# A delta-rule layer in a vision tower: two accumulators for the output's sum, and a new order of the projections and transfers ahead of the recurrence

## What is computed

```python
q = silu(x @ Wq)                       # (b, n, h, hd)
k = silu(x @ Wk); k = k * rsqrt(sum(k * k, -1) + 1e-12)
v = x @ Wv
beta = 2.0 * sigmoid(x @ Wbet); a = sigmoid(x @ Wf)
def step(S, inp):                      # scan over the 64 tokens
    Sd = a * S
    u = v - k . Sd
    S = Sd + beta * outer(k, u)
    o = q . S
o = o * rsqrt(mean(o * o, -1) + 1e-6) * norm_w
return o @ Wo
```

## Time and profile before

| | us |
|---|---|
| median of three runs | 1399.51 (1390.93 to 1405.37) |
| the profiled execution | 1405.84, its span 1404.2 |
| last expert result, first row of this layer on DVE | 570.41, 576.43 |
| first DVE product of the recurrence (L1640) | 666.64 |
| last state ready, DVE's last-token product (L1652) | 962.46 |
| busy: PE, DVE, ACT, POOL | 1163.6, 807.8, 586.9, 521.8 |

### The profile page before, as it was taken

The page is one execution under the profiler, slowest core; times in us unless marked ns, Lnnn a source line. Parts: engine busy times, 40 slices in busy tenths (PEclk is TensorE's granted clock), DMA queues, the critical chain, the costliest instruction groups (busy, mean ns, idle before and its releaser), DMA issues. The chain is left out here.

```text
span 1404.2 us, 24940 instructions
## 1 busy us (share of the span) xinstructions
PE 1163.6 (83%) x9227; PEld 896.1 (64%) x9227; DVE 807.8 (58%) x1850; ACT 586.9 (42%) x1468; POOL 521.8 (37%) x565
## 2 busy tenths in 40 slices
PE   6999984799999999676788888885799999867854
PEld 4666663798999999432455656554577777645543
DVE  3666666211122221545989898996467767532886
ACT  3544452111212121254667667672234444424544
POOL 0111111232333332333687777873112222120657
PEclk9999995799999999899999999997699999979875
DMA  4111100898888886486000000002000031026601
GB/s 146 32 46 46 35 9 12 318 346 333 333 316 329 320 321 240 120 213 173 1 1 0 1 1 1 1 1 74 13 9 11 12 140 50 2 86 253 199 20 57
DMA packets 83352, 162.24 MB, mean 116 GB/s; under 512 B 44128, under 2 KB 62176, under 8 KB 77216
## 3 DMA queue, kind: packets, MB, share of 16 engines
q1 hardware_dynamic: 55536, 111.23, 23.2%
q0 software_dynamic: 10512, 45.10, 8.5%
q10 hardware_dynamic: 17184, 4.33, 1.5%
HBM read 134.28 MB, written 26.35 MB: 114 GB/s over the span
## 5 line engine op out<-in xcount | busy, mean ns | idle before, releaser
L1431 PEld LDWEIGHTS banks<-ys,ident 128*128 128x128 f32 x1008 | 127.3, 191 | 122.3 <-issue 118.3
L922 PE MATMUL banks<-rowsT,w_up 128*128 128x128 f32 x1716 | 202.5, 279 | 0.2 <-DMA w_up<-in_up_w 0.2
L922 PEld LDWEIGHTS banks<-rowsT,w_up 128*128 128x128 f32 x1716 | 199.3, 196 | 0.4 <-DMA w_up<-in_up_w 0.4
L1697 POOL TENSOR_TENSOR ys<-xT_d,q_by_time 128x1024 f32<-128x1024 f32 x63 | 149.0, 2364 | 63.7 <-ACT xT_d L1513 63.7
L1431 PE MATMUL banks<-ys,ident 128*128 128x64 f32 x1008 | 135.0, 289 | 44.7 <-ACT chain_o L1517 43.5
L1422 PE MATMUL banks<-made,ident 128*128 128x512 f32 x256 | 136.8, 616 | 14.6 <-DVE made L1645 14.5
L1542 ACT ACTIVATE banks<-banks,rate 128x256 f32<-128x256 f32 x256 | 104.0, 444 | 91.8 <-DVE made L1640 91.8
L1091 DVE TENSOR_TENSOR hT<-banks,silu 64x128 f32<-64x128 f32 x39 | 11.0, 283 | 170.5 <-ACT silu L979 170.5
L936 PE MATMUL banks<-w_down,hT 128*128 128x256 f32 x468 | 107.5, 379 | 0.6 <-DVE res L1101 0.6
L1640 DVE TENSOR_TENSOR made<-banks,ka 128x512 f32<-128x512 f32 x128 | 87.9, 687 | 23.6 <-PE banks L1422 20.9
L1643 DVE TENSOR_REDUCE banks<-made 128x32 f32<-128x544 f32 x128 | 93.2, 728 | 4.4
(11 more groups left out here) (313 smaller groups left out, 2349.2 us busy)
## 6 DMA issues: line engine op xcount, KB each, us to landing
w_up<-in_up_w SPq DMA_DIRECT2D x39, 1408.0 KB, 5.9
w_down<-in_down_w POOLq DMA_DIRECT2D x39, 768.0 KB, 5.4
inter<-res_x SPq DMA_DIRECT2D x16, 512.0 KB, 3.1
back<-inter SPq DMA_DIRECT2D x15, 512.0 KB, 3.9
patches<-in_patches SPq DMA_DIRECT2D x16, 384.0 KB, 3.2
f<-in_f SPq DMA_DIRECT2D x6, 1024.0 KB, 11.4
ys<-token_rows SPq DMA_DIRECT2D x16, 256.0 KB, 2.8
xn_rows<-xn_all SPq DMA_DIRECT2D x16, 128.0 KB, 1.7
```

Of the source, the lines that this page charges most:

```text
L922: ins = pe.matmul(out[:, m * P:(m + 1) * P], w[:, c, m * P:(m + 1) * P], x[:, c, :], start=(c == 0), stop=(c == 1))
L1431: ins = pe.matmul(o_sum, ident[:, :], products[t % 2][:, :, :, n], start=(n == 0), stop=(n == FOLDED - 1))
L1697: pool.tensor_tensor(qs[:, :, :, :], Sc[(t + 1) % 2][:, :, :, :], bcast(qt[:, t, :, :], 2, HD), ALU.mult).then_inc(sem("qs_made"), 1)
```

## The change

Nine edits, all around this layer:

- `o_sum` has two banks, 5 and 7, used in turns, and `sum_folded(t)` waits for `o_made` t-1 in place of t. The last chunk of squares moves to bank 6; DVE's `mean_square` waits for all three chunks.
- `ticks` goes; PE's and ACT's order are written out. Keys of group g+1 are projected ahead of the queries of group g.
- The first group is projected tile by tile (`project_tile`, 12 products of 128x128).
- The rates are computed in four pieces of 32 partitions, so that the bank holds 128x128 and not 32x512. One store and one load a group replace two and two.
- All stores go by SP, interleaved with the last row loads. ACT issues none.
- The root of the keys' sums is one POOL instruction on 128x64 (`root`, power -0.5), in place of eleven on DVE.
- `square_keys(3)` comes ahead of `turn_queries(2)` on ACT.
- The last group's values and queries are loaded by SP; its queries are turned by POOL (`last_turned`), for which DVE no longer waits at the start but at its last product.
- The rates' weights are interleaved on the host, and `rates` in DRAM is laid out to match.

```diff
-    rates = nc.dram_tensor("rates", (CG, 2, IMAGES // CG, HEADS, TOK), F32).ap()
+    rates = nc.dram_tensor("rates", (CG, IMAGES // CG, HEADS, 2, TOK), F32).ap()
...
-            "rate_made": sb("rate_made", [2 * HEADS, ng])}
+            "rate_made": sb("rate_made", [P, P])}
...
-    o_sum = banks[:, 5, 0:CG * HD].rearrange("p (g v) -> p g v", g=CG)
+    o_sum = [banks[:, b, 0:CG * HD].rearrange("p (g v) -> p g v", g=CG) for b in (5, 7)]
...
-        return banks[:, 6 + n // 2, CG * CUTS[n]:CG * CUTS[n + 1]].rearrange("p (g t) -> p g t", g=CG)
+        return banks[:, 6, CG * CUTS[n]:CG * CUTS[n + 1]].rearrange("p (g t) -> p g t", g=CG)
...
-        return banks[0:2 * HEADS, 1, :]
-
-    def ticks(steps, last):
-        for tick in range(last):
-            for lag, per, count, step in steps:
-                if tick >= lag and (tick - lag) % per == 0 and (tick - lag) // per < count:
-                    step((tick - lag) // per)
+        return banks[:, 1, 0:P]
...
+        def store_pair(first, g):
+            store_made(sp, g, first)
+            store_made(sp, g, first + 1)
+
+        def store_rates(g):
             sp.wait_ge(sem("rate_made"), g + 1)
-            for kind in range(2):
-                sp.dma_start(rates[g, kind, :, :, :].rearrange("b h t -> h b t"),
-                             rate_made[kind * HEADS:(kind + 1) * HEADS, :].rearrange("h (b t) -> h b t", t=TOK)
-                             ).then_inc(sem("rate_stored"), 16)
-            load_chain(sp, g, "k", k)
-            sp.wait_ge(sem("rate_stored"), 32 * g + 32)
-            for kind in range(2):
-                sp.dma_start(rate[:, g, kind, :], rates[g, kind, :, :, :].rearrange("b h t -> (b h) t")
-                             ).then_inc(sem(f"rates{g}"), 16)
-
+            sp.dma_start(rates[g].rearrange("(b j) h n t -> (j h n) b t", b=2),
+                         rate_made[:, :].rearrange("p (b t) -> p b t", b=2)).then_inc(sem("rate_stored"), 16)
+
+        def load_rates(g):
+            sp.wait_ge(sem("rate_stored"), 16 * g + 16)
+            sp.dma_start(rate[:, g, :, :].rearrange("p n t -> p (n t)"),
+                         rates[g].rearrange("b h n t -> (b h) (n t)")).then_inc(sem(f"rates{g}"), 16)
...
+        queries, keys, values = 0, 2, 4
         all_sent(sp)
         for t in range(YS):
             load_rows(t)
-        for t in range(T - YS):
+        for t in range(8):
             next_rows(t)
-        for g in range(CG):
-            send_keys(g)
+        store_pair(keys, 0)
+        next_rows(8)
+        store_pair(values, 0)
+        next_rows(9)
+        store_pair(queries, 0)
+        store_rates(0)
+        next_rows(10)
+        next_rows(11)
+        load_chain(sp, 0, "k", k)
+        load_rates(0)
+        store_pair(keys, 1)
...
+        store_pair(keys, 3)
+        store_rates(3)
+        store_pair(queries, 2)
+        load_chain(sp, 3, "k", k)
+        store_pair(values, 3)
+        load_rates(3)
+        store_pair(queries, 3)
+        load_chain(sp, 3, "v", v)
+        load_chain(sp, 3, "q", q)
...
+        def project_tile(t):
+            at = slice(t * P, (t + 1) * P)
+            pe.wait_ge(sem("xT_copied"), t + 1)
+            for m in (2, 3, 4, 5, 0, 1):
                 for c in range(DC):
                     ins = pe.matmul(banks[:, 2 + m, at], w[:, c, m * P:(m + 1) * P], xT[0][:, c, at],
                                     start=(c == 0), stop=(c == 1), skip_group_check=True)
-                if half:
...
+        def rate_sums(g, copied):
+            pe.wait_ge(sem("xT_copied"), copied)
+            if g:
+                pe.wait_ge(sem("rate_made"), g)
             for c in range(DC):
-                ins = pe.matmul(rate_bank(), w_rate[:, c, :], xT[g % 2][:, c, :], start=(c == 0), stop=(c == 1))
+                images = xT[g % 2][:, c, :].rearrange("p (b j t) -> p j b t", b=2, j=NT)
+                for j in range(NT):
+                    rows = slice(2 * HEADS * j, 2 * HEADS * (j + 1))
+                    ins = pe.matmul(rate_bank()[rows, :].rearrange("p (b t) -> p b t", b=2), w_rate[:, c, :],
+                                    images[:, j, :, :], start=(c == 0), stop=(c == 1), skip_group_check=True)
             ins.then_inc(sem("rate_sums"), 1)
...
-                if t:
-                    pe.wait_ge(sem("o_made"), t)
+                if t > 1:
+                    pe.wait_ge(sem("o_made"), t - 1)
             for n in range(FOLDED // 2 * h, FOLDED // 2 * (h + 1)):
-                ins = pe.matmul(o_sum, ident[:, :], products[t % 2][:, :, :, n], start=(n == 0),
+                ins = pe.matmul(o_sum[t % 2], ident[:, :], products[t % 2][:, :, :, n], start=(n == 0),
...
+        turn(0)
+        turn(1)
+        project_tile(0)
+        turn(2)
+        project_tile(1)
+        turn(3)
+        project_tile(2)
+        turn(4)
+        project_tile(3)
+        turn(5)
+        turn(6)
+        turn(7)
+        rate_sums(0, 8)
+        project(2, 1)
+        project(3, 1)
+        turn(8)
+        turn_past_rates(9, 0)
+        project(4, 1)
+        turn(10)
+        project(5, 1)
+        turn(11)
...
+        project(2, 3)
+        project(3, 3)
+        rate_sums(3, 16)
+        project(0, 2)
+        project(1, 2)
+        project(4, 3)
+        project(5, 3)
+        project(0, 3)
+        project(1, 3)
...
-                if first != 2:
-                    for m in (first, first + 1):
-                        store_made(act, g, m)
...
-            act.copy(o[:, :, :, t], o_sum).then_inc(sem("o_made"), 1)
+            act.copy(o[:, :, :, t], o_sum[t % 2]).then_inc(sem("o_made"), 1)
...
+        keys(3)
+        square_keys(2)
+        rates_of(3)
+        queries(2)
+        values(3)
+        turn_queries(1)
+        queries(3)
+        square_keys(3)
+        turn_queries(2)
...
-            once.mark(dve.tensor_scalar(n2[:, g, :], n2[:, g, :], 1e-12, None, ALU.add))
-            once.settle()
-            x, y = n2[:, g, :].bitcast(I32), rn[:, g, :].bitcast(I32)
-            once.mark(dve.tensor_scalar(y, x, 1, None, ALU.logical_shift_right))
-            once.settle()
-            once.mark(dve.tensor_scalar(y, y, -1.0, float(0x5F3759DF), ALU.mult, ALU.add))
-            once.settle()
-            for _ in range(3):
-                newton(n2[:, g, :], rn[:, g, :], tmp[:, g, :])
+            dve.tensor_scalar(n2[:, g, :], n2[:, g, :], 1e-12, None, ALU.add).then_inc(sem("k_summed"), 1)
...
+            dve.wait_ge(sem("k_root"), g + 1)
...
-            dve.wait_ge(sem("o_summed"), n + 1)
+            dve.wait_ge(sem("o_summed"), CHUNKS_O)
...
+        def root(g):
+            pool.wait_ge(sem("k_summed"), g + 1)
+            pool.tensor_tensor(rn[:, g, :], n2[:, g, :], minus_half[:, 0:1].to_broadcast([P, TOK]), ALU.pow
+                               ).then_inc(sem("k_root"), 1)
...
+        load_chain(pool, 2, "q", q)
+        root(3)
+        scale_keys(3)
+        pool.wait_ge(sem(f"chain_q{CG - 1}"), 16)
+        pool.tensor_copy(qt[:, :, CG - 1, :].rearrange("p t d -> p d t"), q[:, CG - 1, :, :]
+                         ).then_inc(sem("last_turned"), 1)
+        pool.wait_ge(sem("last_turned"), 1)
+        pool.wait_ge(sem("q_turned"), CG - 1)
...
-        "rate_w": rows(np.concatenate([a("L1_attn_Wbet"), a("L1_attn_Wf")], 1)),
+        "rate_w": rows(np.stack([a("L1_attn_Wbet"), a("L1_attn_Wf")], 2).reshape(D, 2 * HEADS)),
```

More of the change, by code:

```diff
@@ L1524, in square_out @@
                        o[:, :, :, CUTS[n]:CUTS[n + 1]]).then_inc(sem("o_squared"), 1)
-        ticks([(0, 1, T, norm), (1, 1, T, copy_xT), (5, 4, CG, made_of(2, ACT.Silu)), (5, 4, CG, rates_of),
-               (6, 4, CG, made_of(4, ACT.Copy)), (7, 4, CG, made_of(0, ACT.Silu)), (9, 4, CG, square_keys),
-               (12, 4, CG, turn_queries)], T + 9)
+        norm(0)
+        norm(1)
+        copy_xT(0)
+        norm(2)
+        copy_xT(1)
+        norm(3)
+        copy_xT(2)
+        norm(4)
+        copy_xT(3)
+        norm(5)
+        copy_xT(4)
+        norm(6)
+        keys(0)
+        copy_xT(5)
+        norm(7)
+        copy_xT(6)
+        copy_xT(7)
+        values(0)
+        rates_of(0)
+        queries(0)
+        norm(8)
+        norm(9)
+        keys(1)
+        copy_xT(8)
+        copy_xT(9)
+        norm(10)
+        norm(11)
+        copy_xT(10)
+        norm(12)
+        copy_xT(11)
+        values(1)
+        rates_of(1)
+        norm(13)
+        norm(14)
+        keys(2)
+        square_keys(0)
+        norm(15)
+        copy_xT(12)
+        rates_of(2)
+        queries(1)
+        copy_xT(13)
+        copy_xT(14)
+        square_keys(1)
+        copy_xT(15)
+        values(2)
+        turn_queries(0)
+        keys(3)
[7 more added lines that the diff above has]
+        turn_queries(2)
         act.preload_act_table_set("natural_log_exp_and_others")
@@ L1684, in gpsimd @@
         prepare(pool)
-        for g in range(CG):
-            if g:
-                scale_keys(g - 1)
```

(17 more changed lines are left out.)

100 lines of the change are left out of this document (55 added, 45 removed).

## The result

| | before | changed |
|---|---|---|
| median of 20 runs, us | 1399.29 (1390.93 to 1406.31) | 1393.81 (1388.27 to 1396.55) |
| ratio | | 0.9947 (0.9934 to 0.996) |
| the profiled execution, its span | 1405.84, 1404.2 | 1388.62, 1386.9 |
| first row of the layer | 576.43 | 572.37 |
| first DVE product | 666.64 | 675.30 |

The change gains 0.5%: 7.4 us by the ratio, 5.5 by the medians, where 33 were forecast. The time lies 8 us above the upper end of the range for 8 in 10 (1352 to 1386).

The account below looks back on a forecast made before the run. DVE, held up by PE's output sum, bounds the recurrence; PE and transfers alternate in the front. 1405.84 - 21.3 (banks) - 12.1 (front) = 1372.4, or 1366 us against 1399.51; own range 1356 to 1377, 8 in 10 1352 to 1386.

Parts of the forecast that it names:

- Two banks: Recurrence: PE's output sum no longer waits for ACT's copy, a step falls from 4.56 to 4.18 us; 21.3 us gained.
- deduction for the squares: Recurrence: four of nine steps with squares' sums keep their old period, taking 1.5 us off the banks' 22.8 us.
- the wait passes on to POOL: Rival, recurrence: PE's sum still waits for POOL's fold and half the gain stays, 1377 us; chance 0.08.
- little comes of it: Rival: front and recurrence both disappoint, or the bank's copy was not the step's limit; 1394 us, chance 0.06.
- The price of the root: Front's end: one POOL root on 64 columns takes 2.5 us, between 0.86 and 45, replacing DVE's 2.8 us.
- fourth rival: Front: POOL's root is paid by the column, four in a row delay the first product; 1457 us, chance 0.07.
- PE's end at 641: Front: PE's last projection product ends at 641 us, within 637.5 to 652.6.
- cost PE nothing: Front: the rates' pieces, eight products of 128 columns a group against two of 512, add no PE time.
- The hole and the half clock: Front: PE's 3.9 us idle before the second group and 2.8 us lost to lower clock, laid to ACT's stores, disappear.
- Transfers at 0.93: Front: 53.8 us of full DMA work from about 594.3 at a 0.93 share ends at 652.1; at 0.84, 658.4.
- Two floors of one height: Front's end: PE's path and the transfers both allow about 652; first product taken at 654.5, 12.1 us gained.
- The row loads: Front: SP's rows 13 to 15, behind stores, may come some 3 us late, but PE reaches them long after.

Follow-up runs that it names:

- e2: The kernel before with two banks for the output's sum and nothing else: 1379.71 us, ratio to before 0.9841.
- e5: e1 with POOL powers and products on 1 to 256 columns of scratch data added behind the recurrence: run once, 1436.1 us.
- e3: The kernel before with the keys' root as one POOL instruction in place of DVE's eleven, nothing else: 1419.44 us, ratio to before 1.0135.
- e1: The changed kernel with the keys' root back on DVE, all else kept: 1362.36 us, ratio to before 0.9736.
- e9: e1 with the last group's `kb` shared, 10 of 16 columns of each head on POOL and 6 on DVE: 1365.38 us, ratio to before 0.9734.
- e7: e1 with the first group projected in two halves again, not tile by tile: 1371.46 us, ratio to before 0.9783.
- e8: e1 with the last group's queries turned by ACT and waited for before the recurrence: 1369.87 us, ratio to before 0.9771.
- e6: e1 with the values' and queries' stores issued by ACT again: 1362.61 us, ratio to before 0.9716.
- e10: e1 with POOL's last `kb` computed twice, one after the other: 1369.98 us, ratio to before 0.9767.

## Why the prediction was wrong, step by step

- **Two banks: right.** 21.3 us forecast; the recurrence shows 21.6, and e2, the banks alone, 21.7. The deduction for the squares was too small: four steps were to keep their old period, and 8 keep a wait, at 4.6 to 4.9 us a step. The other 52 steps x 0.38 give 19.8, so some 2 of the 21.6 us came from elsewhere, and the total is nearer than its terms. The rivals "the wait passes on to POOL" and "little comes of it" fall: POOL is what PE's sum waits for, and DVE does not feel it.
- **The price of the root: wrong, and the cause of the miss.** "I take 2.5 us, nearer to the low end, since a single column carries the whole start of an instruction." It is 10.55 us. The one-column row is 0.71 us, of which about 0.16 is the column (e5), so most of it is a start, as I said; but a column's 0.16 us, 63 times over, is 10 us. I had bounds of 0.86 and 45 us, could not tell between them, and took a value at the low end with the words "nobody needs that many passes for a root". No row stood behind that. The edit alone, on the kernel before, costs 15.9 us of front (e3), and taken out of the changed kernel it gives back 28.4 (e1). By the factor of two that the Trainium skill ("GPSIMD Engine Reference", section on performance versus the Vector engine) gives for elementwise work, the estimate was 5.5 us: the right direction, and half of the cost.
- **The fourth rival's mechanism: right; the closeness of its date is luck.** It said 617 + 4 x root + 4 x 3.83 + 0.4. With 10.55 that is 674.9; the first product came at 675.30. But the first root began at 612.95 and not 617, and a root and its `kb` take 15.7 us and not 14.4, because DVE's scaling and POOL's issues of loads stand between them. The two errors, -4.1 and +4.5 us, cancel. Its break-even was 8.5 us for the front and 13.9 for the whole change, and 10.55 lies between: the front loses, the recurrence more than pays for it. The mechanism had a chance of 0.07, and I priced it only at 28 us a root, where it makes the kernel slower. The case that came, between the two limits, had no place among the rivals, though its sign ("if POOL's root is over 8 us, the fourth rival holds") was on the list. Two of its figures are off by little: the second break-even comes to 13.8, and the time at 28 us to 1456.
- **PE's end at 641: too late by 9.5 us.** It was 631.5. The layer began 4.1 us earlier (572.37); over all kernels that date ran from 570.0 to 576.4, and e1 and e9, alike up to there, began at 572.6 and 576.1, so it is no effect of the front's edits. Most of the rest can be the rates: "cost PE nothing" was wrong in the other direction. Their sum takes 0.64 us and not 1.90, 4 x 1.26 = 5.0 us in all. The hole and the half clock went as forecast; tiles brought about 1 us and not 3 (e7), so a further 2 us were gained that none of these terms names. No run has the rates' pieces alone.
- **Transfers at 0.93: too low.** The share was 1.01 from 594 to 641, where it was 0.84 before. Two floors of one height was right in e1 to 1.3 us: the last eviction ended at 634.8, and the keys' load let the squares go at 636.13. But PE sets neither. It was done at 631.7, and the last two evictions had waited 2.54 and 0.30 us for stores of queries.
- **The front with the root on DVE** took 74.5 and 75.0 us. I had forecast 90.2 - 12.1 = 78.1 with a root of 2.5 us. All else that I sized in the front came out 3 us better than I said, and the root 8 us worse, four times over. Which edits made the front's 15 us is shown in part only: the turned queries some 3 (e8), the tiles 1 (e7), the issuer of the stores nothing (e6). The order of the projections, the rates' pieces and the place of the row loads were not taken apart.
- **The row loads** of SP: DVE waited for them 12.0 us in 4 waits, against 5.6 in one before. e1 has the same order and a front of 74.5 us, so they cost nothing that kept the front from its gain; what the order would give without these waits was not tried.
- **The time itself.** By the stages of the two profiled executions: +12.7 front, -21.6 recurrence, -4.3 in the rest at a slightly higher clock, -4.1 ahead of the layer: -17.3. The ratio of 20 runs says -7.4 (5.6 to 9.2 less). The edited stages alone give -8.9, which agrees with it. The other 8 us lie in stages without an edit: the profiled execution of before was 6.5 us above its median of 20 runs, that of the change 5.2 us below its own.

## What to carry to other kernels

A single instruction in place of eleven is no gain if each column of it is paid dearly. Before a power goes to GpSimd, its price at the real width has to be in a row, or the forecast has to give both ends of the bound a fair chance; a one-column row can't tell the start from the column. Where work moves to an engine that serves every group in turn, write down that engine's own list as a chain, start + n x (old work + new work + what stands between them), and solve it for the price at which it passes the old end. And a wait marked "DMA" is to be followed to the engine that issues the transfer.

## What the runs showed of the hardware that I had not expected

- POOL's power costs 0.57 us for one column of 128 partitions and 0.16 us for each further one, up to 41.12 us for 256; a product of 256 columns takes 0.61 us.
- POOL and DVE slow each other when DVE reads both operands from SBUF: `kb` 3.83 us beside `ka`, 2.36 us without it (e10), and DVE's 384 columns 2.10 us beside POOL's `kb` where 0.71 were due (e9). The end dates fit one waiting for the other to within 0.25 us. Beside DVE's products with an operand in a bank POOL's product of 1024 columns took 2.36 us.
- Sixteen passes of 128 columns into four pieces of 32 partitions took 0.64 us, where the four passes of 512 columns into one piece took 1.90: the columns are as many, so passes into different partitions of the output seem to have overlapped. That is inferred from the time alone.
- The last stage, with the same work, took from 437.4 to 446.7 us at a granted clock of 0.87 to 0.85.
